# Probabilities transposed on VectorE, values in 32x64 tiles, and 64x128 tiles for the scores of the widest key block

## What is computed

```python
# layer 0 (x = in_x) and layer 1 (x = what layer 0 gives)
xn = layernorm(x) * g_in
q = (xn @ Wq), 16 heads of 64; k, v = halves of xn @ Wkv, one for all heads
k, v = concat(null, k), concat(null, v)            # 129 keys
# layer 1 only: q and k scaled to length one, times learned scales, times 8
sim = q @ k^T + bias                               # layer 0: given; layer 1: from a small network
sim = where(later key or masked key, -max, sim)
out = softmax(sim) @ v                             # 16 heads x 128 x 64
x = x + layernorm(out @ Wo) * g_out
```

## Time and profile before

| what | us |
|---|---|
| median of 3 runs (lowest to highest) | 2316.56 (2315.45 to 2318.55) |
| the profiled execution's own time | 2315.64 |
| its span, first to last instruction | 2313.9 |
| TensorE busy | 2264.6 |
| VectorE, ScalarE, GpSimd busy | 1610.4, 1599.8, 911.3 |
| granted clock of TensorE, mean of the span | 0.994 |

### The profile page before, as it was taken

How to read it: one execution, slowest core, us unless ns; L and a number is a source line. 1 busy time by engine, 2 the same in 40 slices (tenths; PEclk the granted TensorE clock), 3 DMA queues, 4 the chain that set the end, 5 groups by cost and what they waited for, 6 DMA issues and landing times.

```text
span 2313.9 us, 63351 instructions
## 1 busy us (share of the span) xinstructions
PE 2264.6 (98%) x21531; PEld 1972.1 (85%) x21531; DVE 1610.4 (70%) x4513; ACT 1599.8 (69%) x6497; POOL 911.3 (39%) x1702
## 2 busy tenths in 40 slices
PE   5899999999999999999999999999999999999998
PEld 5688888888888888888888888888888888888877
DVE  6667677667667677676676776676676676766766
ACT  5667767667667667776677676676676777666766
POOL 3334334434433433443343344344334334334432
PEclk8999999999999999999999999999999999999999
DMA  7111121111121111111111211111211111111111
GB/s 248 41 50 51 46 62 45 54 58 43 54 62 44 49 57 48 53 55 47 54 54 42 62 46 52 58 44 53 62 44 49 57 47 53 58 47 50 59 40 39
DMA packets 107255, 129.56 MB, mean 56 GB/s; under 512 B 45664, under 2 KB 49840, under 8 KB 107216
## 3 DMA queue, kind: packets, MB, share of 16 engines
q1 hardware_dynamic: 105472, 127.92, 18.0%
q0 software_dynamic: 688, 1.14, 0.3%
q10 hardware_dynamic: 1056, 0.00, 0.0%
HBM read 81.79 MB, written 33.57 MB: 50 GB/s over the span
## 4 chain that ended last, share of the span: by engine, by line
PE 83%; ACT 7%; DVE 5%; SPq 2%; issue 1%; POOL 1%; DMA 0%; DVEq 0%; POOLq 0%
PE psum L722 26%; PE psum L582 15%; PE psum L614 12%; PE psum L708 10%; PE psum L673 7%; PE psum L685 5%; ACT probs L878 4%; PE psum L631 3%; PE psum L539 2%; PE psum L593 2%; DVE probs L1087 2%; SPq L391 1%; DVE neg_max L1094 1%; DVE q_sb L1073 1%; ACT norm_inv L863 1%
## 5 line engine op out<-in xcount | busy, mean ns | idle before, releaser
L1370 POOL TENSOR_TENSOR weights<-probs,den_inv 128x256 f32<-128x256 f32 (+3 forms) x1024 | 471.1, 487 | 1353.3 <-DVE den_inv L1100 1349.3
L878 ACT ACTIVATE probs<-probs,neg_max 128x129 f32<-128x129 f32 (+3 forms) x2048 | 715.9, 352 | 285.9 <-DVE neg_max L1094 283.9
L1357 POOL TENSOR_TENSOR masked_bias<-bias,pad_neg 128x516 f32<-128x516 f32 (+3 forms) x512 | 396.3, 807 | 13.7 <-POOL pad_neg L1353 4.9
L1087 DVE TENSOR_TENSOR probs<-psum,masked_bias 128x324 f32<-128x324 f32 x512 | 225.5, 482 | 235.3 <-PE psum L673 235.3
L878 ACT ACTIVATION_READ_ACCUMULATOR probs<-probs,neg_max 128x1 f32 x2048 | 384.4, 188 | 0.0
L722 PE MATMUL psum<-wo_hi,o_hi 128*128 128x512 f32 x1024 | 271.5, 407 | 0.8 <-issue 0.8
L722 PE MATMUL psum<-wo_hi,o_lo 128*128 128x512 f32 x1024 | 268.0, 403 | 1.3 <-DVE o_lo L1105 1.3
L1094 DVE TENSOR_REDUCE neg_max<-probs 128x2 f32<-128x258 f32 (+3 forms) x1024 | 256.7, 312 | 4.4
L722 PE MATMUL psum<-wo_lo,o_hi 128*128 128x512 f32 x1024 | 259.6, 395 | 0.0
L885 ACT COPY probs_t<-psum 128x384 f32<-128x384 f32 (+1 forms) x512 | 192.6, 428 | 60.2 <-PE psum L685 60.0
L722 PEld LDWEIGHTS psum<-wo_lo,o_hi 128*128 128x128 f32 x1024 | 192.2, 188 | 46.6
(11 more groups left out here) (138 smaller groups left out, 4193.8 us busy)
## 6 DMA issues: line engine op xcount, KB each, us to landing
res<-in_x_dram SPq DMA_DIRECT2D x64, 256.0 KB, 2.6
x_of<-y_out SPq DMA_DIRECT2D x64, 256.0 KB, 2.1
res<-x_of SPq DMA_DIRECT2D x64, 256.0 KB, 2.7
out_dram<-y_out SPq DMA_DIRECT2D x64, 256.0 KB, 2.1
xa<-in_x_dram SPq DMA_DIRECT2D x63, 256.0 KB, 2.6
xa<-x_of SPq DMA_DIRECT2D x63, 256.0 KB, 2.8
q_aside<-qp SPq DMA_DIRECT2D x32, 256.0 KB, 2.9
w_raw<-in_L_cond_Wq_dram SPq DMA_DIRECT2D x8, 512.0 KB, 8.8
```

What stands on the lines that cost most here:

```text
L878: x_ = nc.scalar.activation(s, s, ACT.Exp, bias=neg_max[:, g, k, e:e + 1], accum_out=den[:, g, k, e:e + 1])
L1087: a = nc.vector.tensor_tensor(probs[:, 2 * c + e, :], SB[c][e][:, 0:ROW], masked_bias[:, 2 * c + e, :], ALU.add)
L1357: m = nc.gpsimd.tensor_tensor(block(masked_bias, b), block(bias[u.layer], b), pad_neg[u.layer][:, 0:WIDTH[b]].unsqueeze(1).to_broadcast([P ...
L1370: m = nc.gpsimd.tensor_tensor(places[b], block(pairs(probs, g // 2), b)[:, :, 1:1 + n], den_inv[:, g, k, :].unsqueeze(2).to_broadcast([P, ...
```

## The change

Probabilities are divided in place and transposed by VectorE in 32x32 blocks (`turn`, one instruction for each block of rows and half), into `probs_t`, with the 32 keys of a block on 32 partitions. `values` multiplies block by block of keys `k`, in 32x64 tiles: 4 key blocks x 2 heads x 4 strips of partitions, each strip into a bank of its own, 256, 192, 128 and 64 columns. For that every strip needs all values, `v_rep`: 16 copies of 32 partitions a unit from `v_diff`. `transpose_p`, `take_pt`, `weights` and `v_part` go. The scores of the widest block use 64x128 tiles, two matmuls instead of four; the other blocks stay at 64x64. Banks move: Q is banks 0, 1 and 4, the scores' first half 2 and 3, Y is bank 2, the values 4 to 7. With that come new waits: the scores for `y_read` two units back, the output projection for the first added bias (`first_taken`), the transposes of x for `o_lo_done[0]`. VectorE, ScalarE and GpSimd get new orders; GpSimd divides all four groups ahead of the mask. The diff, cut:

```diff
-        Q = [psum[:, b, :] for b in range(3)]
-        SP = [psum[:, 3 + b, :] for b in range(2)]
-        O = [psum[:, 5 + b, :] for b in range(2)]
-        Y = psum[:, 7, :]
+        Q = [psum[:, b, :] for b in (0, 1, 4)]
+        SP = [psum[:, 2 + b, :] for b in range(2)]
+        O = [psum[:, 4 + t, :] for t in range(4)]
+        Y = SP[0]
+        H_T, HW, DIAG = O[1], O[3], SP[1]
 
         SB = (SP, Q[0:2])
-        TILES = ((0, 1, 2), (3, 4))
 
 ...
             def copy_v(n):
-                sp.dma_start(v_part[n][3 * R:P, 1, :], v_diff[n][0:R, :]).then_inc(v_part_loaded[n], 16)
-                sp.dma_start(v_part[n][DH:P, 3, :], v_diff[n][0:DH, :]).then_inc(v_part_loaded[n], 16)
-
-            def copy_unit_v(w):
-                wait_apart(sp, v_ready, w.sdone * 3, sp_passed)
+                for t, strip in enumerate(strips):
+                    for k, keys_of in enumerate(strips):
+                        sp.dma_start(v_rep[n][strip, k, :], v_diff[n][keys_of, :]).then_inc(v_rep_loaded[n], 16)
+
+            def copy_unit_v(w, v):
+                wait_apart(sp, v_ready, w.sdone, sp_passed)
+                wait_apart(sp, values_done, v.done, sp_passed)
                 copy_v(side(w)[0])
 
-            def copy_pair_v(w):
-                if static(w.even, 0, 0):
-                    sp.wait_ge(v_part_zeroed, 3)
-                wait_apart(sp, pair_v_ready, w.pdone * 6, sp_passed)
+            def copy_pair_v(w, v=None):
+                wait_apart(sp, pair_v_ready, w.pdone * 2, sp_passed)
+                if v:
+                    wait_apart(sp, values_done, v.done, sp_passed)
                 copy_v(0)
                 copy_v(1)
 ...
-                run_stages((copy_keys, w), (part(finish, u), v), (copy_pair_v, w))
+                run_stages((copy_keys, w), (part(finish, u), v), (part(copy_pair_v, v if u.layer else u), w))
 
             def late(u, v, w, n, loads, then, pairs_done):
-                run_stages((load_xa, loads[0] if loads else None), (load_keep_behind, then), (copy_unit_v, w),
+                run_stages((load_xa, loads[0] if loads else None), (load_keep_behind, then), (part(copy_unit_v, v), w),
                            (load_xa, loads[1] if len(loads) > 1 else None), (part(finish, u), v))
 ...
+            def transpose_second(w, v):
+
+                wait(pe, o_lo_done[0], v.done)
                 transpose_x(w)
 ...
-                    for g in (2, 3):
-                        wait(pe, pt_copied[g], u.prev)
+                    wait(pe, y_read, u.before)
 ...
                 for b in (3, 2, 1, 0):
-                    for r in range(0, P, TR):
+                    tr = P if b == BLOCKS - 1 else TR
+                    for r in range(0, P, tr):
                         for e in range(2):
                             half = slice(e * DH, (e + 1) * DH)
                             k = keys[half, 0:WIDTH[b]] if u.layer else (kv_t, k_high)[e][half, u.odd, 0:WIDTH[b]]
-                            m = nc.tensor.matmul(block(SB[c][e], b)[r:r + TR, :], queries(u, c, half, b)[:, r:r + TR], k,
+                            m = nc.tensor.matmul(block(SB[c][e], b)[r:r + tr, :], queries(u, c, half, b)[:, r:r + tr], k,
                                                  start=True, stop=True)
 ...
-            def transpose_p(u, groups):
 ...
             def values(u):
                 n, filled = side(u)
 ...
+                wait(pe, v_rep_loaded[n], filled * 16 * BLOCKS * 4)
+                wait(pe, o_lo_done[1], u.prev)
+                for g in range(NG):
+                    wait(pe, turned[g], u.done)
+                if not isinstance(u.done, int):
+                    pe.sem_inc(pe_passed, 1)
+                for k in range(BLOCKS):
+                    for e in range(2):
+                        for t, strip in enumerate(strips):
+                            o = O[t][e * DH:(e + 1) * DH, 0:2 * P].rearrange("p (c i) -> p c i", c=2)[:, :, k * R:]
+                            m = nc.tensor.matmul(o, v_rep[n][strip, k, :],
+                                                 probs_t[strip, :, e, k, k:, :].rearrange("p c b i -> p c (b i)"),
+                                                 start=(k == 0), stop=(k == BLOCKS - 1))
+                m.then_inc(values_done, 1)
+
+            def project_out(u, p, now=None):
                 if p == 0:
                     for b in range(2):
                         wait(pe, o_hi_done[b], u.done)
                     wait(pe, y_read, u.prev)
+                    if now:
+                        wait(pe, first_taken, now.done)
                 if p == 2:
 ...
             def late(u, v, w, n, loads, then, pairs_done):
 ...
+                if u:
+                    scores(u, 0)
+                    scores(u, 1)
+                if w:
+                    transpose_second(w, v)
+                project_out(v, 0, u)
+                project_out(v, 1)
+                if w:
+                    project(w, u)
+                project_out(v, 2)
+                if w:
+                    transpose_k(w)
+                    transpose_q(w)
+                    wait(pe, keys_ready, w.sdone)
+                if u:
+                    if not w:
+                        wait(pe, o_lo_done[0], u.prev)
+                    values(u)
 ...
-            def take_pt(u, groups):
 ...
+                    if e == 1:
+                        a.then_inc(biased[c], 1)
+                    elif c == 0:
+                        a.then_inc(first_taken, 1)
 ...
+            def turn(u, groups):
+                for g in groups:
+                    wait(dve, probs_done[g], u.done)
+                    c = g // 2
+                    for b in GROUPS[g % 2]:
+                        m = nc.vector.transpose(probs_t[:, c, :, 0:b + 1, b, :],
+                                                block(pairs(probs, c), b)[:, :, 1:].rearrange("p e (k r) -> p e k r", r=R))
+                    m.then_inc(turned[g], 1)
+
+            def split_o(u, f):
+                wait(dve, o_hi_done[f], u.done)
+                part_of = lambda t: t[:, f * D:(f + 1) * D].rearrange("p (t i) -> p t i", t=2)
+                nc.vector.scalar_tensor_tensor(part_of(o_lo), psum[:, 4 + 2 * f:6 + 2 * f, 0:2 * P], null_v_col[:, 0:1],
+                                               part_of(o_hi).bitcast(F32), ALU.add, ALU.subtract).then_inc(o_lo_done[f], 1)
 ...
             def first(u, v, w, n, then):
 ...
+                input_statistics(w.odd)
+                split_o(v, 0)
+                add_bias(u, 0)
+                row_max(u, (0, 1))
+                add_bias(u, 1)
+                split_x(w.even)
+                normalise(w.odd)
+                inverse_sum(u, (0,))
+                row_max(u, (2, 3))
+                inverse_sum(u, (1,))
+                split_o(v, 1)
+                split_x(w.odd)
+                turn(u, (0,))
+                inverse_sum(u, (2,))
+                turn(u, (1,))
+                inverse_sum(u, (3,))
+                start_finish(v)
+                turn(u, (2,))
+                end_finish(v)
+                turn(u, (3,))
+                input_statistics(n)
+                normalise(n)
 ...
             def second(u, v, w, n, then):
 ...
+                split_o(v, 0)
+                add_bias(u, 0)
+                row_max(u, (0, 1))
+                add_bias(u, 1)
+                split_o(v, 1)
+                inverse_sum(u, (0,))
+                row_max(u, (2, 3))
+                inverse_sum(u, (1,))
+                turn(u, (0,))
+                inverse_sum(u, (2,))
+                start_finish(v)
+                turn(u, (1,))
+                inverse_sum(u, (3,))
+                take_kvt(w)
+                turn(u, (2,))
+                end_finish(v)
+                turn(u, (3,))
+                take_pair_v(w)
+                input_statistics(n)
 ...
             def late(u, v, w, n, loads, then, pairs_done):
 ...
+                split_o(v, 0)
+                if u:
+                    add_bias(u, 0)
+                    row_max(u, (0, 1))
+                    add_bias(u, 1)
+                    inverse_sum(u, (0,))
+                if w:
+                    split_x(w)
+                if u:
+                    row_max(u, (2, 3))
+                    inverse_sum(u, (1,))
+                split_o(v, 1)
+                if u:
+                    turn(u, (0,))
+                    inverse_sum(u, (2,))
+                    turn(u, (1,))
+                if n:
+                    input_statistics(n)
+                if u:
+                    inverse_sum(u, (3,))
+                if w:
+                    take_v(w)
+                    norms(w, 2)
+                if u:
+                    turn(u, (2,))
+                if w:
+                    unit_q(w, 2)
+                    norms(w, 0)
+                if n:
+                    normalise(n)
+                if w:
+                    unit_q(w, 0)
+                if u:
```

(20 more changed lines are left out.)

244 lines of the change are left out of this document (107 added, 137 removed).

## The result

The changed kernel takes 2972.35 us (median of 4 runs, 2969.74 to 2976.79) against 2316.72 us, measured beside it (2315.45 to 2318.55): 1.283 times the time, 95% interval 1.281 to 1.285. The profiled execution took 2971.8 us, its span is 2968.8. The forecast was 2890, in a range of 2580 to 3000.

The account below looks back on a forecast made before the run. TensorE bounds the kernel before; after the change, SP's queue delays loads of x. 2315.6 us plus 537 (30 x 17.9), 30 for the clock and about 8 for first and last slots gives 2890, range 2580 to 3000.

Parts of the forecast that it names:

- What bounds it: SP's queue: 32 and 16 copies at 0.62 us delay loads of x; second `late` +12.4 us, `first` +5.3.
- rival A: SP's queue: issuing copies is cheap and doesn't hold SP; 71.0 us a pass, about 2350 us; chance 0.05.
- the clock: TensorE at half clock after long waits in second `late`, mostly hidden under SP's copies: 1 us a pass, 30 in all.
- The head of the slot: Start of `second`: output projection waits for the first bias add, going on at about 2.2 us instead of 1.37.
- the q chain: In `late`, norms and scaling of q stand behind `turn`; transposes of q start at 16.3 to 16.9 us, not 15.3.
- The turn: VectorE's transposes of the probabilities cost 1.84 us a slot, priced like the row maximum; bounds half or twice.
- Rival C: VectorE's four-byte transposes several times dearer; at four times, 5.5 us more a slot, above 3000 us; chance 0.05.
- The values: TensorE's value matmuls, eight tiles side by side, take 1.23 us instead of 1.88; some 2.3 if only four run together.
- The scores: TensorE's scores take 1.80 us a slot instead of 1.37: wide tiles save nothing, three more shape changes cost 0.14 each.
- Rival D: Scores don't get cheaper; 0.43 us a slot, 55 us, but hidden under the slot-head wait; held likely, no number given.
- TensorE alone: TensorE's own work per slot: -1.05 -0.65 +0.43 = -1.27 us, 163 us less over 128 slots.
- Rival B: TensorE stays the bound and is faster, no other engine's work being longer: 2153 us; chance 0.07.

Follow-up runs that it names:

- e9_no_chains: Changed kernel with 6 copies a unit, SP's queue reordered and the widest block's scores in 64x64 tiles, other engines' orders as changed: 2332.28 us, 1.0070 times the kernel before.
- the fastest run: Changed kernel with 6 copies a unit, SP's queue reordered, widest block's scores in 64x64 tiles, TensorE, VectorE and ScalarE reordered: 2191.58 us, 0.9460 times the kernel before.

## Why the prediction was right, and where it was short

**What bounds it: right.** SP's queue, by 32 and 16 copies ahead of loads, in the two slots named. Copies came at 0.633 us, I had 0.62. The Trainium skill (DMA: Bandwidth & Descriptors, Issuing engines are not separate DMA queues), by which the time to initiate a DMA is usually small beside the DMA itself and rival A would hold, doesn't agree with this trace: each copy held SP 0.59 us of the 1.8 until it landed, and 32 of them 20.2.

**The slots, point by point.** Odd `late` 19.1 foreseen, 19.27 came; `second` 16.5 and 16.73; `first` 21.9 and 22.05; second `late` 30.6 and 33.99. That is 92.04 us against 88.1 and 1 for the clock, 2.9 us a pass too little, 88 us over 30 passes; the other slots gave 6 back. The second `late` is the largest miss: its load came 0.8 us later than foreseen, and from the statistics to the slot's end it took 12.5 us instead of 9.9, with TensorE at 0.50 of the clock for the last 9.3.

**The failed term: the clock.** I put 1 us a pass and wrote that most of the loss lies under SP's copies. That fits the second `late`. In `first` the transposes of x and two output chains stand behind the load, at 0.59 of the full clock. From the statistics to the end of `first` it was 18.55 us (2061.86 to 2080.41) where I took 16.2. Of these 2.35 us the clock is 1.67: with the two matmuls more the same stretch takes 16.88 (means of the loop). The run that reordered SP's queue has 16.56, so 0.36 is that 16.2 was too low, and 0.32 no run separates. The rest is SP's again: the second load was issued 34.9 us after the start of the second `late`, where I had 33.6, because the first one went 0.8 us later and the mask row behind it as well; statistics at 37.7, not 36.3. With 0.4 us in the other two slots that is 1.4 + 2.35 + 0.4 - 1.0 = 3.15 us, and the pass shown is 92.27, 3.17 over 89.1.

**The head of the slot and the q chain: right.** In `second` the output projection starts 2.26 us into the slot (2007.40 to 2009.66); 2.2 was said. In the odd `late`, which no load delays, the transposes of q start 16.9 us into it (16.3 to 16.9 was said):

```profile
2005.05 1.06 PE L626 MATMUL psum<-ident,q_sb 128*128 128x128 f32 x8 [1.29 <-DVE q_sb L1087]
```

**The turn: right.** Two of the four groups in `second`, each with the instruction behind it:

```profile
2017.29 0.49 DVE L1124 STREAM_TRANSPOSE probs_t<-probs 128x192 f32<-128x192 f32 x2
2017.71 0.13 DVE L1117 RECIPROCAL den_inv<-den 128x4 f32<-128x4 f32 x1
...
2018.13 0.63 DVE L1124 STREAM_TRANSPOSE probs_t<-probs 128x256 f32<-128x256 f32 x2
2018.68 0.80 DVE L1148 SCALAR_TENSOR_TENSOR y_out<-y_out,rstd_out,res 128x512 f32<-128x512 f32 x1
```

0.42 us from the smaller group to what follows, 0.55 from the larger: 1.94 us a slot where the row maximum gave 1.84. Rival C, which had four times that, is out.

**The values: right in kind.** 1.39 us at the full clock, from this row to the scores at 2024.15; 1.23 was said. Four tiles at a time, at 2.3 us, is refuted, and eight side by side is what comes nearest:

```profile
2022.76 1.42 PE L684 MATMUL psum<-probs_t,v_rep 32*64 32x256 f32 x64
```

**The scores: right result, wrong reason.** They took 1.92 us in the second `late` (2024.15 to 2026.07) against 1.80 said, and hidden. But I had the two wide tiles at the price of the four and all of the loss in changes of shape. The widest block itself takes 0.19 us more a half; the change back to the wide tile between the halves another 0.16 (2024.95 to 2025.11) where a group of 33 columns needs 0.03. Rival D was right in its direction only.

**TensorE alone: too much by the wide tiles.** I said 163 us less. Its busy time falls from 2264.6 to 2152.6 in the run that only reordered SP, 112 us; with 64x64 scores (e9_no_chains) it falls to 2088.1, 176 us. Rival B, that TensorE stays the bound and the kernel gets faster, needed more than SP's relief, as the prediction said of the q chain: reordered copies alone end at 2350, which is what the walk gave for rival A. With the chains shortened and 64x64 scores as well, 2191.6 is 39 us from B's 2153.

## What to carry to other kernels

Count the issues on each DMA queue, price each by the row of one of its kind, and see which load stands behind them; of the 656 us lost here, moving the same 48 copies behind the loads gave back 622. Where a wait on TensorE grows, cost the work behind it at the lower clock if that work is on the path: in `first` 6.80 us instead of 4.22. A change that fails for a reason beside its idea is worth a second look: the transposes on VectorE and the 32x64 values are 5.4% faster than the kernel before once the copies are fewer and out of the way, `late` is reordered and the scores keep their 64x64 tiles. Order alone can't have done that, as its 2191.6 us are less than TensorE's busy time before, 2264.6.

## What the chip showed that I had not expected

- A copy from SBUF to SBUF of 32, 64 or 96 partitions held SP 0.55 to 0.60 us in the rows shown, whether it moved 1 KB or 24; a load of 256 KB from DRAM held it 0.33.
- TensorE's loop kept its code up to 1713 instructions a pass, as the trace records them (the fastest run: 26 packets on the instruction queue in the whole execution). At 1814 and 1990 it took 279 and 281 packets, and TensorE stood still 3.8 and 4.0 us, on average, at the start of `first`, where the loop goes back to its beginning. The Trainium skill (Runtime: NRT & Kernel Launch, Instruction fetch mechanics) gives TensorE's instruction memory 128 KiB or 2048 instructions and calls a refill mostly hidden, but for a taken branch out of the fetched window, which stalls. The traces don't speak against the size, as 4.60 MB against 0.41 is some 150 KB for each of 28 returns of the loop, and the stall stands where such a branch is. SP's copies came every 0.66 us in the first of these runs and every 0.68 to 0.71 in the second, on average, against 0.64 in the change; that the refill slowed them is an inference from the two standing together.
- A pass of a 64x128 tile with 129 columns takes 0.19 us, as long as its own load of weights (0.18 to 0.19; a 64x64 tile's 0.13). By the Trainium skill (TensorE: Matmul & The Clock Gate, LDWEIGHTS) a weight load goes by its columns, and the rows here go the same way; that the load sets the pace of the pass was not tried.
- Two matmuls of 512 columns, ahead of a gap that had been 3.1 us and was 1.4 with them, left the transposes and the two output chains behind it at the full clock: 4.2 us (1486.69 to 1490.91) instead of 6.8.
